# A GraphSAGE block on one NeuronCore: two maxima spread by PE with a diagonal, the weight squares in other places of PE's order, and eight counts moved to the last self feature

## What is computed

```python
deg_inv = 1.0 / jnp.maximum(deg, 1.0)
def _sage_layer(h, edge_src, edge_dst, deg_inv, W_self, W_neigh, b):
    msg = h[edge_src]
    agg = jax.ops.segment_sum(msg, edge_dst, num_segments=h.shape[0])
    mean = agg * deg_inv[:, None]
    return h @ W_self + mean @ W_neigh + b
h = jax.nn.relu(_sage_layer(x, ..., W_self0, W_neigh0, b0))
out = _sage_layer(h, ..., W_self1, W_neigh1, b1)
x = _layernorm(x + out, axis=-1)
```

## Time and profile before

| | us |
|---|---|
| median of three runs | 691.9 |
| the profiled execution, whole | 688.98 |
| its span, first to last instruction | 687.3 |
| PE matmul busy | 647.4 (94% of the span) |
| DVE busy | 384.5 (56%) |
| ACT busy | 198.1 (29%) |
| POOL busy | 118.6 (17%) |
| chain that ended last: PE's share | 87% |

### The profile page before, as it was taken

The page is one execution under the profiler, slowest core; times in us unless marked ns, Lnnn a source line. Parts: engine busy times, 40 slices in busy tenths (PEclk is TensorE's granted clock), DMA queues, the critical chain, the costliest instruction groups (busy, mean ns, idle before and its releaser), DMA issues.

```text
span 687.3 us, 11585 instructions
## 1 busy us (share of the span) xinstructions
PE 647.4 (94%) x3400; PEld 334.8 (49%) x3400; DVE 384.5 (56%) x1001; ACT 198.1 (29%) x349; POOL 118.6 (17%) x196
## 2 busy tenths in 40 slices
PE   3589989997999999999999999999899999999995
PEld 3544545543566666555555444444344444444442
DVE  7687487869977776268789855341033222323223
ACT  5472824344343444113336401231100000000000
POOL 4001336632333333100000000000041111001100
PEclk9699999999999999999999999999999999999998
DMA  8606000000000000060000510000311111110100
GB/s 320 242 1 244 2 0 0 0 1 0 1 1 2 0 0 0 3 246 1 0 0 0 195 50 1 0 0 0 94 46 47 62 61 61 61 60 32 54 31 23
DMA packets 11394, 33.42 MB, mean 49 GB/s; under 512 B 1976, under 2 KB 2136, under 8 KB 11360
## 3 DMA queue, kind: packets, MB, share of 16 engines
q1 hardware_dynamic: 11360, 32.99, 13.2%
HBM read 27.87 MB, written 5.12 MB: 48 GB/s over the span
## 4 chain that ended last, share of the span: by engine, by line
PE 87%; issue 4%; DVE 3%; ACT 1%; POOL 0%; POOLq 0%; DVEq 0%; ACTq 0%
PE ps L517 26%; PE ps L629 15%; PE ps L544 15%; PE ps L650 13%; PE ps L581 12%; PE ps L462 4%; PE ps L595 1%; DVE scratch L907 1%; DVE lohot L905 1%; DVE xz L940 1%; PE ps L489 1%; POOL A L377 0%; DVE ws L245 0%; PE ps L474 0%; ACT scratch L675 0%
## 5 line engine op out<-in xcount | busy, mean ns | idle before, releaser
L517 PE MATMUL ps<-wn,xz 128*128 128x512 f16 x480 | 118.0, 385 | 3.4 <-DVE wn L245 3.4
L544 PE MATMUL ps<-xz,ws 128*128 128x420 f16 (+1 forms) x576 | 114.8, 339 | 0.0
L629 PE MATMUL ps<-wn,zh 128*128 128x512 f16 x480 | 105.4, 379 | 2.1 <-issue 2.1
L907 DVE TENSOR_SCALAR scratch<-iota_q,table 125x240 f16<-125x240 f16 x320 | 104.8, 327 | 0.1
L517 PE MATMUL ps<-ws,zh 128*128 128x512 f16 x480 | 103.8, 379 | 0.0
L905 DVE TENSOR_SCALAR lohot<-iota_lo,table 125x128 f16<-125x128 f16 x320 | 88.3, 276 | 20.9 <-PE ps L462 20.2
L377 POOL TENSOR_TENSOR A<-A,scratch 128x120 int32 x160 | 72.2, 451 | 135.7 <-ACT scratch L675 104.1
L675 ACT ACTIVATE scratch<-ps 128x240 uint16<-128x240 f32 x160 | 58.6, 370 | 111.1 <-PE ps L462 88.8
L650 PE MATMUL ps<-xz,A 128*128 128x512 f16 x400 | 88.0, 379 | 0.0
L581 PE MATMUL ps<-A,zh 128*128 128x420 f16 (+1 forms) x480 | 84.7, 340 | 0.0
L629 PEld LDWEIGHTS ps<-wn,zh 128*128 (+1 forms) x480 | 46.8, 98 | 59.3 <-issue 3.1
(11 more groups left out here) (122 smaller groups left out, 432.4 us busy)
## 6 DMA issues: line engine op xcount, KB each, us to landing
ws<-in_L_gnn_W_neigh SPq DMA_DIRECT2D x8, 1024.0 KB, 12.8
zh<-in_x SPq DMA_DIRECT2D x9, 512.0 KB, 8.5
ws<-in_x SPq DMA_DIRECT2D x9, 512.0 KB, 3.2
out<-ws SPq DMA_DIRECT2D x18, 256.0 KB, 2.2
ws<-in_L_gnn_W_self SPq DMA_DIRECT2D x4, 1024.0 KB, 8.8
wn<-in_L_gnn_W_self SPq DMA_DIRECT2D x4, 1024.0 KB, 8.1
ws<-in_L_gnn_b SPq DMA_DIRECT2D x1, 512.0 KB, 4.7
zh<-in_x SPq DMA_DIRECT2D x1, 392.0 KB
```

The lines of the kernel that those rows point to most:

```text
L517: ins = pe.matmul(ps[0:TP, 2 * r + half, :], lhs(a, k, t), w[:, k, b, half * HD:(half + 1) * HD], start=(k == 0 and a == 0 and b == 0), st ...
L544: ins = pe.matmul(ps[:, b, 0:CH[n]], ws[:, k, a, bass.ds(f * P, P)], xT[h][:, k, CO[n]:CO[n] + CH[n]], start=(k == 0 and a == 0 and h == 0 ...
L629: ins = pe.matmul(ps[0:TP, g + half, :], zh[:, k, a, bass.ds(t * TP, TP)], wn[:, k, b, half * HD:(half + 1) * HD], start=(k == 0 and a == ...
L907: ins = dve.tensor_scalar(qhot[0:EP, r, k, :], iota_q[0:EP, :], q[0:EP, b, bass.ds(row, 1)], None, ALU.is_equal)
```

## The change

- **Spreading by PE.** For x and for wn0, DVE multiplies the unit matrix by the maxima (or by the matrix of squares), which leaves them on a diagonal; PE multiplies a matrix of ones by it, so every partition gets all 128 values as a row in PSUM; DVE takes the maximum of the row. POOL's spreads of x and wn0 are gone; its first one is now b0's.
- **PE's order in the front** is written out: turns 0 to 2, x's spread, `gram` of blocks 0 to 3, turn 3, blocks 4 and 5, turns 4 and 5, blocks 6 and 7, turn 6, wn0's spread, turns 7 to 9.
- ACT makes eight high parts of x instead of nine ahead of wn0's split, the other two behind it. DVE makes one group of one-hots ahead instead of two.
- **Tile 1** has no counts in steps 0 to 3 and two a step in steps 4 to 7.
- **Tile 9** has eight groups instead of sixteen; ws0's blocks 5, 6, 7 are split behind copies 1, 3, 5 (before 3, 4, 5), and DVE makes their low parts behind one-hots 2, 4, 6 (before 10, 11, 12 of sixteen). All later groups move up by eight, and the last eight go with f = 0, chunk n = 2, one a step, which is now done ahead of the wait for the last copy. Chunks 0 and 1 stay behind it.

```diff
-    EARLY = 2
+    EARLY = 1
     FRONT = 7
-    FIRST = GT * JT
+    FIRST = GT * (JT - 1)
...
-        return GT * t - GT, 2 * GT if isinstance(t, int) and t == JT - 1 else GT
+        return GT * t - GT, GT
...
+            pool.wait_ge(A_zeroed, 1)
             spread(0)
-            spread(1)
-            pool.wait_ge(A_zeroed, 1)
-            spread(2)
             adds(0)
             adds(1)
-            spread(3)
+            spread(1)
             adds(2)
...
+            def spread_diag(m):
+
+                pe.wait_ge(diag_ready, m + 1)
+                pe.matmul(ps[:, 7, m * P:(m + 1) * P], ones[:], diags[:, m, :], start=True,
+                          stop=True).then_inc(diag_spread, 1)
+
+            for j in range(3):
+                turn(j)
+            spread_diag(0)
+            gram(0)
+            gram(2)
+            turn(3)
+            gram(4)
+            turn(4)
+            turn(5)
+            gram(6)
+            turn(6)
+            spread_diag(1)
+            for j in range(7, JT):
+                turn(j)
...
-                        for g in range(k * n // KT, (k + 1) * n // KT):
+                        late = KT // 2 if isinstance(t, int) and t == 1 else 0
+                        for g in range(max(k - late, 0) * n // (KT - late), max(k + 1 - late, 0) * n // (KT - late)):
...
+            self_part(0, 2, SELF[2], NG - 3 * GT, 0, 3 * GT)
...
             pe.wait_ge(counts_copied, nwin * NG)
-            for n in range(3):
+            for n in range(2):
                 self_part(0, n, SELF[n], 0, 0, 0)
...
-            for j in range(JT - 1):
+            for j in range(FRONT + 1):
                 xhigh(j)
...
-                                if g in (3, 4, 5):
-                                    split(splits, KT - 6 + g)
+                                if g in (1, 3, 5):
+                                    split(splits, KT - 3 + g // 2)
...
-            xhigh(JT - 1)
+            for j in range(FRONT + 1, JT):
+                xhigh(j)
...
+            def spread_max(name, m):
+
+                dve.wait_ge(diag_spread, m + 1)
+                link(dve.tensor_reduce(c("all" + name), ps[:, 7, m * P:(m + 1) * P], AX.X, ALU.max))
...
-            tensor_max("x", JT, 0)
+            link(dve.tensor_reduce(c("maxx"), mx[:, 0:JT], AX.X, ALU.max))
+            dve.tensor_scalar(diags[:, 0, :], ident[:], c("maxx"), None, ALU.mult).then_inc(diag_ready, 1)
             ahead(0, EARLY)
-            scale("x")
+            spread_max("x", 0)
+            pow2("x", c("allx"))
+            link(dve.tensor_scalar(c("s_x"), c("r_x"), 8192.0, None, ALU.mult))
...
-            link(dve.tensor_tensor(squares, ps[:, 6, 0:P], ident[:], ALU.mult))
-            dve.tensor_reduce(c("maxwn0"), squares, AX.X, ALU.max).then_inc(maxes_ready, 1)
+            dve.tensor_tensor(diags[:, 1, :], ps[:, 6, 0:P], ident[:], ALU.mult).then_inc(diag_ready, 1)
             xlow(FRONT - 1)
-            dve.wait_ge(max_spread, ORDER.index("wn0") + 1)
+            spread_max("wn0", 1)
...
-            z_tile(JT // 2 - 1, 1, lambda g: low_part(dve, "ws0", g - 5) if g in (10, 11, 12) else None)
+            z_tile(JT // 2 - 1, 1, lambda g: low_part(dve, "ws0", g // 2 + 4) if g in (2, 4, 6) else None)
```

More of the change, by code:

```diff
@@ L53, in gnn_kernel @@
     KEPT = KT - 1
-    FIRST = GT * JT
+    FIRST = GT * (JT - 1)
     MORE = 3 * GT
-    assert FIRST + GT + (KEPT - 1) // 2 * MORE == NG
+    assert FIRST + 2 * GT + (KEPT - 1) // 2 * MORE == NG
     SAME = 7
@@ L139, in raw @@
             return w[:, k + 1:k + 1 + n].rearrange("p k h d -> p k (h d)").bitcast(F32)
+        diags = wn[:, KT].rearrange("p h d -> p (h d)").bitcast(F32)[:, 0:2 * P].rearrange("p (i c) -> p i c", i=2)
         rounded = scratch[0:TP, 0:NPAD]
@@ L180, in gnn_kernel @@
         gram_ready = sem("gram_ready")
+        diag_ready = sem("diag_ready")
+        diag_spread = sem("diag_spread")
         cs_ready = sem("cs_ready")
@@ L227, in gnn_kernel @@
         WN = {"wn0": (wn, ws, Wn0), "ws0": (ws, ws, Ws0), "wn1": (ws, ws, Wn1), "ws1": (wn, wn, Ws1)}
-        ORDER = ["x", "wn0", "b0", "ws0", "wn1", "h", "ws1"]
+        ORDER = ["b0", "ws0", "wn1", "h", "ws1"]
         SPLIT = ["wn0", "ws0", "wn1", "ws1"]
@@ L424, in _ @@
                             add(w * NG + RING * i + r, r, False, w * (WIN // 2))
-            spread(4)
+            spread(2)
             pool.wait_ge(unit_ready, 3 * (KT - 1))
             pool.memset(zh[:, 0:KT, :, N:NP], 0.0).then_inc(h_tail_zero, 1)
-            spread(5)
-            spread(6)
+            spread(3)
+            spread(4)
             pool.wait_ge(b1_in, 16)
@@ L477, in gram, with turn @@
                     ins.then_inc(gram_ready, 1)
-            for j in range(JT):
+            def turn(j):
                 pe.wait_ge(x_in[j], 16)
@@ L483, in _ @@
                 if j == JT - 1:
-                    pe.wait_ge(maxes_ready, 2)
+                    pe.wait_ge(scale_ready, 2)
                 elif j >= 3:
@@ L491, in _ @@
                 ins.then_inc(panel_ready, 1)
-                if 2 <= j < 2 + KT // 2:
-                    gram(2 * j - 4)
+            def spread_diag(m):
[16 more added lines that the diff above has]
+                turn(j)
             def panel(i, r, lhs, w, layer):
@@ L767, in _ @@
                     keep(2 * v + u - 1, v * MORE + (FIRST + GT - MORE), u * MORE // 2, MORE // 2)
+            for g in range(GT):
+                take(NG - GT + g, g % RING, RING)
             act.wait_ge(table_ready, 1)
@@ L957, in _ @@
             dve.wait_ge(gram_ready, 1)
-            squares = wn[:, KT].rearrange("p h d -> p (h d)").bitcast(F32)[:, 0:P]
-            link(dve.tensor_tensor(squares, ps[:, 6, 0:P], ident[:], ALU.mult))
-            dve.tensor_reduce(c("maxwn0"), squares, AX.X, ALU.max).then_inc(maxes_ready, 1)
+            dve.tensor_tensor(diags[:, 1, :], ps[:, 6, 0:P], ident[:], ALU.mult).then_inc(diag_ready, 1)
             xlow(FRONT - 1)
-            dve.wait_ge(max_spread, ORDER.index("wn0") + 1)
+            spread_max("wn0", 1)
             root = c("t_wn0").bitcast(I32)
@@ L1051, in _ @@
                             v * (MORE // GR) + (FIRST + GT - MORE + g) // GR)
+            for g in range(GT):
+                onehots(NG - GT + g, g, (NG - GT + g) // GR)
             def groups(i, extra):
```

## The result

The changed kernel took 683.08 us (median of 6 runs, 680.4 to 684.91) against 691.94 for the kernel before on the same chips: ratio 0.9869, interval 0.9845 to 0.9892, so 8.9 us or 1.3% faster. 689.4 was forecast, with a range down to 686.5.

A forecast was written before the change was run, and what follows sets the result against it. PE was taken to bound all that the change touches; +0.7 for the front with POOL, -5.1 for tile 9 and +1.9 for the last counts made -2.5, so 691.9 became 689.4, range 686.5 to 692.0.

The forecast's parts named there:

- PE loses time in three places here: Whole kernel: PE loses time in the front, waiting for POOL's first add at the ninth count, and in tile 9.
- part 2: POOL's return to the adds: first add at 65.65, PE waits 3.25 at the ninth count; whole front +0.7.
- Part 1: Front up to panel 1: full clock from 28.3, wn0's first split at 36.9 instead of 39.57, -2.7.
- My end for an early rise: Front: if the clock rises two items earlier, the first split gains -3.3 instead of -2.7.
- The rival of a clock that stays low until 31: Front: clock rises only at 31 as before, panel 1 at 52.9, total 691.0; chance 0.09.
- the 64 that I had named as a sign of being wrong: POOL's first add: expected near 65.6; before 64 or after 68 would show the forecast wrong.
- the rival "the load is not slowed": POOL's return: traffic does not slow the library load, first add at 64.5, total 687.05; chance 0.22.
- The rival of first use: POOL's return: the 10.55 belongs to first use of the adds' code, first add 68.1, total 691.9; chance 0.16.
- Part 3: Tile 9: takes 16.2 instead of 21.35, with three waits of 1.1 besides the first of 0.93; -5.1.
- Part 4: Last eight counts under f = 0: +1.7, plus some 0.2 wait for the last copy, cast hidden; +1.9.
- The slower rival: POOL's load makes no progress under traffic, then takes 10.55; first add at 70.3, total 694.05; chance 0.08.

The follow-up runs named there:

- the order alone: Kernel before with only PE's order of turns and squares as in the change, POOL's spreads of both maxima kept: 689.32 us, ratio 0.9974.

## Why the prediction was wrong

**Where PE loses time.** "PE loses time in three places here" is the step that failed. A fourth stood on the page of the kernel before, in the group of line 629:

```profile
L629 PE MATMUL ps<-wn,zh 128*128 128x512 f16 x480 | 105.4, 379 | 2.1 <-issue 2.1
```

I did not price it, since nothing in the diff is near it. The prediction lets what follows the front move along with PE's counts and has no term for the second layer. The change makes PE's program a few instructions longer ahead of that product, and the stop goes: 1.9 to 5.1 by the timed runs, some 3.7, and 2.2 to 4.8 by the profiled ones. It is an accident of placement: 64 unexecuted instructions, put where eight had taken the stop away, brought one at the degrees. By these figures, uncertain by 1.5, it is the larger of two missing pieces. The other is part 2, some 2.9; with the stop's 3.7 put back the time would be 686.8, just inside the range.

**Part 1** (-2.7 forecast, -4.06 in the profile). Right in kind, and beyond the end that was named. The clock rose at 26, not at 28.3: turn 3 took 1.17, not 1.7 to 1.9. The spread by PE was 0.79 for x, where 0.7 was taken. My end for an early rise was -3.3; the second squares also started at 24.14, half a microsecond earlier than I had them. The rival of a clock that stays low until 31 is out.

**Part 2** (+0.7 for front and POOL together; 2.2 gained when measured with the stop in place; in the profile 2.85 at the ninth count and 1.42 at the last count of tile 8). Mis-sized twice. The return to the adds took 7.0 where I had 6.95 + 1.15: a fixed price per us of loads does not hold, as 2.0 of loads cost 0.5 at most and six or seven 3 to 4. The first add at 63.30 lies before the 64 that I had named as a sign of being wrong. Here the rival "the load is not slowed" was the better one: first add 64.5 by it, 63.30 seen, though not because traffic never hurts (9.9 and 7.1 with and without it). The rival of first use is out by the 7.0 and by the 7.1. The figure of about 6 us for a code load (the Trainium skill, GPSIMD Engine Reference, 2.1 Instruction dispatch) put the first add at 63.55, near to what came. That was luck: the change of library stood at 56.3, not at 57.55, and the return took 7.0. No return to the adds here took under 6.8, and beside long loads the traces disagree with the figure by 4 to 5. And the clock did not fall behind the ninth count; it fell at the 25th, where I expected nothing new.

**Part 3** (-5.1): 16.3 seen, 16.2 forecast, with the three waits of about 0.9 in the place of 1.1. **Part 4** (+1.9): 1.7 for the counts, no wait for the last copy that the profile shows, the cast hidden. Together -3.5 measured, -3.2 forecast.

**The sum.** -3.5 for tile 9 and the counts, -2.2 for front and POOL, about -3.7 for the stop: -9.4, against -8.9 for the whole. The split between the last two rests on differences of ratios and is uncertain by 1.5. The profiled executions split their 7.2 in the same order: 1.4 up to tile 9, 3.3 from there to the degrees, 2.5 behind them, where the execution before had the stop without the fall of the clock. The slower rival is out.

## What to carry to other kernels

Price every stop on the bounding engine that the page names "issue", also where the diff is far away: a longer or shorter program ahead of a jump can remove it, bring it or move it, and a few unexecuted instructions show which. So time a kernel that differs by such a shift beside the edit before the gain is put down to the edit. And a change of POOL's library is cheapest when there is none: grouping calls of one library gave 4.3 more than the change itself (0.9 by the profiled executions), which had made the load quicker and waited for it.

## What the runs showed of the hardware that was not expected

- PE stops for 2.0 to 3.4 at a jump or two or three matmuls behind it, depending on where the code behind the jump lies. The Trainium skill (Runtime: NRT & Kernel Launch, Instruction fetch mechanics) says that instructions arrive in blocks of 16 KiB, 256 instructions, and that a taken branch to a place outside the blocks at hand waits for a fetch. The traces agree in part: the runs with 8, 64 and 250 unexecuted instructions fit it, and queue 8 shows packets of 16 KB at the jump; but eleven kernels take the same jumps without a stop of over 0.7.
- Behind a wait or stop of 2 to 3 the granted clock fell in some executions and stayed at 1.00 in others, and the length does not tell them apart. At the 25th count it fell behind 2.30 (the change) and 2.81 (b0's spread moved), not behind 2.55 (before) and 2.75 (250 in the changed kernel, row below). In the second layer it fell behind 2.12, 2.72 and 2.88, not behind 2.04 and 2.09. At a stop of 2 to 3 the fall adds some 1.7. PE's timeline with the 250:

```profile
91.72 0.38 PE L463 MATMUL ps<-scratch,lohot 125*128 125x240 f16 x2 [2.75 <-ACT scratch L701]
```

- The clock rose from 0.50 to its upper level at about 26 in the two kernels where PE takes 32 squares from about 22 on with a gap of 0.4 to 0.7 between the halves (0.98 from 26 to 28 with the change, 1.00 with the order alone). Before, PE waited 3.96 behind the first 16 squares, and the clock rose some 5 us later.
